# A DLRM tower on one core: five chunks of tile 0 stacked by PE and ACT, and gathers 36 to 95 released by DVE's steps

## The reference

```
e = jnp.stack([tbl_0[ids[:, 0]], ..., tbl_38[ids[:, 38]]], axis=1)   # (2048, 39, 32)
p, q = e[:, ROW, :], e[:, COL, :]                                    # 741 pairs
z = jnp.einsum('bpc,apc,bpa->bp', p, w, q)
h = jnp.concatenate([z, dense_ctx], axis=1)
h = jnp.maximum(h @ W_top1 + b_top1, 0.0)
h = jnp.maximum(h @ W_top2 + b_top2, 0.0)
y = h @ W_top3
```

## Time and profile before

| | |
|---|---|
| time, 3 runs | 738.17, 739.40, 740.45 us; median 739.4 |
| the profiled execution | 739.08 us, its span 737.2 us |
| granted TensorE clock, mean of the span | 0.977 |
| instructions of the span | 10924 |
| DMA traffic | 141.40 MB, mean 192 GB/s |

### The profile page before, as it was taken

The page is one execution under the profiler, slowest core; times in us unless marked ns, Lnnn a source line. Parts: engine busy times, 40 slices in busy tenths (PEclk is TensorE's granted clock), DMA queues, the critical chain, the costliest instruction groups (busy, mean ns, idle before and its releaser), DMA issues.

```text
span 737.2 us, 10924 instructions
## 1 busy us (share of the span) xinstructions
PE 678.2 (92%) x4202; PEld 274.6 (37%) x4202; DVE 608.3 (83%) x773; ACT 104.3 (14%) x186; POOL 415.6 (56%) x424
## 2 busy tenths in 40 slices
PE   0678886898997999999999999999999999999998
PEld 0233332333333444434344444433434444343443
DVE  3776797799996998898889997998889978788740
ACT  3423301111110010101211010110110101011002
POOL 5777465567777766567766665567766666000000
PEclk9888999899998999999999999999999999999999
DMA  7644979779876573547675582728686373553200
GB/s 200 209 119 138 334 272 301 252 231 314 284 227 202 195 257 108 166 140 236 224 225 192 202 281 68 240 85 259 194 270 214 125 254 98 179 174 104 97 0 0
DMA packets 72271, 141.40 MB, mean 192 GB/s; under 512 B 13829, under 2 KB 23704, under 8 KB 72092
## 3 DMA queue, kind: packets, MB, share of 16 engines
q1 hardware_dynamic: 48796, 116.86, 46.2%
q10 hardware_dynamic: 9984, 16.94, 6.4%
q0 software_dynamic: 13440, 6.91, 6.4%
HBM read 109.66 MB, written 31.00 MB: 191 GB/s over the span
## 4 chain that ended last, share of the span: by engine, by line
PE 70%; DVE 14%; issue 7%; DMA 4%; POOL 3%; ACT 1%; SPq 0%; DVEq 0%; ACTq 0%
PE u_ps L593 23%; PE z_ps L617 21%; DVE prod L914 9%; PE m_ps L630 8%; PE t_ps L556 7%; DVE one_hot L902 4%; POOL e_rows L422 3%; PE m_ps L632 3%; PE t_ps L537 2%; DMA e<-scratch 1%; DMA e_rows<-in_tbl_dram,idx 1%; PE u_ps L652 1%; PE u_ps L661 1%; PE m_ps L634 1%; PE t_ps L644 1%
## 5 line engine op out<-in xcount | busy, mean ns | idle before, releaser
L422 POOL DMA_INDIRECT e_rows<-in_tbl_dram,idx x420 | 415.4, 989 | 212.9 <-issue 89.9
L914 DVE TENSOR_TENSOR prod<-u_ps,eT 128x1024 f32<-128x1024 f32 x400 | 469.5, 1216 | 77.6 <-PE u_ps L593 77.1
L593 PE MATMUL u_ps<-e,w 128*128 128x512 f32 x800 | 260.9, 437 | 24.6 <-DVE prod L914 14.6
L617 PE MATMUL z_ps<-prod,sel 128*32 128x512 f32 x1600 | 222.9, 614 | 0.0
L593 PEld LDWEIGHTS u_ps<-e,w 128*128 128x128 f32 x800 | 132.2, 190 | 173.4 <-DVE prod L914 85.9
L902 DVE TENSOR_SCALAR one_hot<-hot_idx,row 125x512 bf16<-125x512 f16 (+2 forms) x296 | 107.6, 420 | 9.6 <-PE t_ps L556 5.8
L556 PE MATMUL t_ps<-one_hot,tb 125*32 125x512 bf16 x1344 | 104.2, 392 | 10.5 <-DVE one_hot L902 9.1
L556 PEld LDWEIGHTS t_ps<-one_hot,tb 125*32 125x32 bf16 x1344 | 43.7, 99 | 89.3 <-issue 57.6
L617 PEld LDWEIGHTS z_ps<-prod,sel 128*32 128x32 f32 x1600 | 33.8, 108 | 111.7 <-issue 87.4
L630 PE MATMUL m_ps<-zT,w1s 128*128 128x512 f32 x144 | 73.5, 592 | 0.0
L720 ACT CAST parts<-t_ps 128x512 fp32r<-128x512 f32 (+1 forms) x40 | 23.4, 586 | 295.4 <-PE t_ps L556 162.4
(11 more groups left out here) (52 smaller groups left out, 122.2 us busy)
## 6 DMA issues: line engine op xcount, KB each, us to landing
w<-w_rows SPq DMA_DIRECT2D x100, 512.0 KB
e<-scratch SPq DMA_DIRECT2D x62, 512.0 KB, 5.7
scratch<-parts SPq DMA_DIRECT2D x62, 256.0 KB
w_rows<-h ACTq DMA_DIRECT2D x48, 256.0 KB
e_rows<-in_tbl_dram,idx POOLq DMA_INDIRECT x420
hot_idx<-hot SPq DMA_DIRECT2D x12, 512.0 KB
h<-in_w_dram ACTq DMA_DIRECT2D x12, 256.0 KB, 4.3
e<-scratch SPq DMA_DIRECT2D x8, 384.0 KB
```

The source lines that it names most:

```text
L422: pool.indirect_dma_start(e_rows[:, r, n, D * q:D * q + D], None, tables[f], bass.IndirectOffsetOnAxis(ap=idx[:, t, f * TPG + n:f * TPG + ...
L593: last = nc.tensor.matmul(u_ps[:, s % 2, place, :], w4[:, p % WR, (u % PW) * P:(u % PW + 1) * P], e4[:, E4_SLOT[g], j - C * g, :], start=T ...
L617: last = nc.tensor.matmul(z_ps[D * quad:D * quad + D, z % 2, :], sel[:, D - 1 - row:2 * D - 1 - row], prod[:, (NS * t + n) % PR, place, :] ...
L914: nc.vector.tensor_tensor(prod[:, s % PR, :, :], u_ps[:, s % 2, :, :], e, ALU.mult).then_inc(s_mul, 1)
```

## The change

Two edits.

1. In tile 0 the stacks of chunks 4, 8, 5, 6 and 9 are no longer stored and read back. PE makes them field by field, one field a batch, from the batches in `FIELD_WISE`, in the bank `m_ps`, and ACT copies each to `e4`. 19 fields: 38 matmuls, 19 copies. Five pairs of stores and five pairs of stack DMAs of SP go. `make_field` stands in PE's order between the batch's `interact` and its `reduce`; it waits for `split_chunk`, and for ACT's copy of the field before it (the bank). `take_field` stands in ACT's order before the batch's `take_z`, `take_chunk` and the weights.
2. Gathers 36 to 95 wait for DVE's steps (36 steps for 60 gathers, from step 1 on) instead of the landing of the gather three before. The rule for the later ones starts from there: gather 96 waits for 37 steps done, 45 before, gather 143 for 80, 88 before, and so on, always 8 fewer.

```diff
@@ -119,8 +119,18 @@
 WR = 4
 ES = 4
 
-PACED_FROM, PACE_LEAD = 96, 52
+PACED_FROM, PACED_FIRST, STEPS_FIRST = 36, 60, 36
 GATHERS_PER_TILE = 108
+
+
+def gather_step(n):
+
+    n -= PACED_FROM
+    if n < PACED_FIRST:
+        return 1 + n * STEPS_FIRST // PACED_FIRST
+    return 1 + STEPS_FIRST + (n - PACED_FIRST) * NS // GATHERS_PER_TILE
+
+
 
 E4_SLOT = {0: 0, 1: 2, 2: 3, 3: 1, 7: 2, 8: 3, 4: 0, 5: 1, 6: 0, 9: 1}
 OS = 3
@@ -151,6 +161,9 @@
 
 MADE = ((0, 1), (0, 0), (0, 2), (0, 3), (0, 7))
 MADE_FIRST = 2
+
+FIELD_WISE = {(0, 4): 9, (0, 8): 15, (0, 5): 21, (0, 6): 30, (0, 9): 35}
+STACKED = MADE + tuple(FIELD_WISE)
 MADE_IN = {1: (((0, 2), 0), ((0, 2), 1)), 4: (((0, 3), 0), ((0, 3), 1)), 5: (((0, 7), 0),), 6: (((0, 7), 1),)}
 MLP_WEIGHTS_BATCH = 7
 LATE = (17, 39)
@@ -189,7 +202,22 @@
 
 def stores_to(n):
 
-    return len([m for m in range(n + 1) if (m - n) % 2 == 0 and ORDER[m] not in MADE])
+    return len([m for m in range(n + 1) if (m - n) % 2 == 0 and ORDER[m] not in STACKED])
+
+
+def stk_at(c, part):
+
+    earlier = STACKED[:STACKED.index(c)]
+    return sum(2 if x in MADE else fields_in(x[1]) for x in earlier) + part + 1
+
+
+def stk_after(c):
+    return stk_at(c, (2 if c in MADE else fields_in(c[1])) - 1)
+
+
+def field_in(b):
+
+    return [(c, b - first) for c, first in FIELD_WISE.items() if first <= b < first + fields_in(c[1])]
 
 
 def halves_before(c, half):
@@ -230,7 +258,7 @@
     INDICES.setdefault(LAST_SLICE.get(LOOKED[LPOS[c] - 2], -1) + 1, []).append(c)
 for b, cs in COMPLETE.items():
     for c in cs:
-        if c in MADE:
+        if c in STACKED:
             continue
         x = e4_before(c)
         free = NBAT * x[0] + J_LAST[x[1]] // UPB + 1 if x else 0
@@ -418,7 +446,7 @@
                             before = issued - WINDOW
                             pool.wait_ge(s_rows[GPOS[GATHERS[before]] % ER][before % WINDOW], landed(before))
                         if issued >= PACED_FROM:
-                            pool.wait_ge(s_mul, PACED_FROM - PACE_LEAD + 1 + (issued - PACED_FROM) * NS // GATHERS_PER_TILE)
+                            pool.wait_ge(s_mul, gather_step(issued))
                         pool.indirect_dma_start(
                             e_rows[:, r, n, D * q:D * q + D], None, tables[f],
                             bass.IndirectOffsetOnAxis(ap=idx[:, t, f * TPG + n:f * TPG + n + 1], axis=0),
@@ -573,6 +601,18 @@
                     for h in range(2):
                         last = nc.tensor.matmul(to, rep[own, 2 - 2 * h:2 - 2 * h + P], parts[own, n % 2, h, :],
                                                 start=h == 0, stop=h == 1)
+                last.then_inc(s_stk, 1)
+
+            def make_field(c, q):
+
+                n = POS[c]
+                pe.wait_ge(s_el, n + 1)
+                d = c if q else STACKED[STACKED.index(c) - 1]
+                pe.wait_ge(s_e4[E4_SLOT[d[1]]], 32 * e4_loads(d) - (32 - 8 * q if q else 0))
+                own = slice(D * q, D * q + D)
+                for h in range(2):
+                    last = nc.tensor.matmul(m_ps[:, :], rep[own, 2 - 2 * h:2 - 2 * h + P], parts[own, n % 2, h, :],
+                                            start=h == 0, stop=h == 1)
                 last.then_inc(s_stk, 1)
 
             def interact(t, n):
@@ -683,6 +723,9 @@
                 for b in range(NBAT):
                     for x in range(SPB):
                         interact(t, SPB * b + x)
+                    if t == 0:
+                        for c, q in field_in(b):
+                            make_field(c, q)
                     if t:
                         for piece in mlp_pieces(b, t == NT - 1):
                             mlp_piece(t - 1, *piece)
@@ -709,8 +752,8 @@
                 n = POS[c]
                 rows = D * fields_in(g)
                 if n >= 2:
-                    if ORDER[n - 2] in MADE:
-                        act.wait_ge(s_stk, 2 * MADE.index(ORDER[n - 2]) + 2)
+                    if ORDER[n - 2] in STACKED:
+                        act.wait_ge(s_stk, stk_after(ORDER[n - 2]))
                     else:
                         act.wait_ge(s_scr[n % 2], 32 * stores_to(n - 2))
                 if hot(c):
@@ -726,7 +769,7 @@
 
             def take_half(c, half):
                 made = MADE.index(c)
-                act.wait_ge(s_stk, 2 * made + half + 1)
+                act.wait_ge(s_stk, stk_at(c, half))
                 x = e4_before(c)
                 if x:
                     act.wait_ge(s_u, step_after(*x))
@@ -736,6 +779,13 @@
                 else:
                     nc.scalar.copy(e4[:, slot, q, :], m_ps[:, :]).then_inc(s_e4[slot], 8)
                     nc.scalar.copy(e4[:, slot, q + 1, :], z_ps[:, 1, :]).then_inc(s_e4[slot], 8)
+
+            def take_field(c, q):
+                act.wait_ge(s_stk, stk_at(c, q))
+                act.wait_ge(s_u, step_after(*e4_before(c)))
+                slot = E4_SLOT[c[1]]
+                rest = 8 if q < fields_in(c[1]) - 1 else 32 - 8 * q
+                nc.scalar.copy(e4[:, slot, q, :], m_ps[:, :]).then_inc(s_e4[slot], rest)
 
             def load_weights(k):
                 a, b = PREP_UNITS[k]
@@ -831,6 +881,9 @@
                         for layer, m, k in mlp_pieces(b, t == NT - 1):
                             if k == LAYER_INPUTS[layer] - 1:
                                 take_mlp(t - 1, layer, m, m_ps[:, :])
+                    if t == 0:
+                        for c, q in field_in(b):
+                            take_field(c, q)
                     for tile in range(NZ):
                         done = ends_tile(tile) // UPB + 1
                         if done == b:
```

## The result

The changed kernel took 734.99 us (median of 20 executions, 730.74 to 740.52); the kernel before, timed beside it, 738.29 (20 executions, 734.78 to 741.08). The ratio is 0.9957, interval 0.9937 to 0.9977: 3.3 us, 0.4% faster. The forecast was 732.3, so less than half of the 7.1 us came. Two executions of the last set of experiments, of 885.82 and 910.98 us, were in a slower state at a lower granted clock, and its medians leave them out. The profiled execution of the changed kernel took 733.83 us (span 732.0), 5.2 us less than the profiled one of before.

A forecast was written before the change was run, and what follows sets the result against it. PE was taken to bound tiles 1 to 3, so only tile 0's idle time could pay. Terms -6.3 - 5.6 + 1.0 + 3.2 + 0.6 = -7.1 us from 739.4 gave 732.3 us, range 727.0 to 737.5.

The forecast's parts named there:

- Rival 1: Tile 0's fields fully exposed, 10.5 instead of 3.2 us: 739.6, half exposed 736; chance 0.12, and 0.03 beyond 739.
- Rival 2: Only one stop goes, another wait replacing it ((1, 0)'s stack or (1, 3)'s gather): price 2.5 to 5.6 us; chance 0.07.
- The two stops: Tile 0, PE's waits at batch 19 (chunk 8's stack) and batch 48 (gather 143) go: -6.3 and -5.6 us.
- The gathers' edit: Gathers 36 to 95 by DVE's steps end POOL's landing waits, so the second stop, batch 48, goes: -5.6 us.
- I count nothing: Some 7 MB of SP's traffic go, spare for the weight loads; counted as 0.
- What is late next: At the second stop, step 100 waits for the stack of (1, 0), still through DRAM: 0 to 4 us, taken as +1.0.
- The fields: 19 fields on PE at 0.55 us, 10.5 us, partly hidden in PE's idle time in batches 9 to 37: +3.2 us exposed.
- ACT's casts: Weight casts stand behind ACT's field copies, so DVE waits, mainly in batches 17 and 37: +0.6 us, bounds 0 and 3.
- The low clock: Low clock after the first stop counted as 0.8 us of its gain; little clock cost expected at the second.
- rival 3: ACT, standing at its weight loads in batches 11, 19, 23, blocks PE's fields: up to +17.2 us, 749.5; chance 0.05.
- Rival 4: More comes than counted, by lighter DMA load and fields at 0.33 us: 728.2, down to 727; chance 0.13.

The follow-up runs named there:

- stacks_only: The changed kernel with only the first edit: five stacks by PE and ACT, gathers as in the kernel before; 734.84 us, ratio 0.9954 to before.
- both_again: The changed kernel, both edits, run once more for a second profile and the granted clock of every timed run; 734.15 us, ratio 0.9956 to before.
- stacks_with_traffic: First edit only, but SP still stores and reads back the five chunks, into memory nobody reads; 737.68 us, ratio 1.0000 to before.
- chunk8_gathers: Changed kernel with both edits, but only chunk 8 made by PE and ACT, chunks 4, 5, 6, 9 through DRAM; 732.25 us, ratio 0.9921 to before.
- chunk8_only: Only chunk 8's stack by PE and ACT, the other four through memory, gathers as in the kernel before; 735.22 us, ratio 0.9968 to before.
- gathers_only: The kernel before with only the second edit: gathers 36 to 95 by DVE's steps, all stacks as before; 734.79 us, ratio 0.9950 to before.

## Why the prediction was right, and where it was wrong

The time lies in the range (727.0 to 737.5) and just inside the forecast's own band, 729.5 to 735. It lies there with some luck: that side of the range was opened for rivals 1 and 2, and neither of them is what took the gain.

**The two stops, right.** -6.3 and -5.6 were forecast, -6.5 and -5.0 measured.

**The gathers' edit, right in effect, wrong in credit.** The step "POOL was late, because of 25 waits for landings" was right; the step that only the second edit ends them was wrong. The same text said that 7 MB of traffic go while the DMA share is 0.87 to 0.98, and "I count nothing". With the stacks alone the waits fell from 33.0 to 19.2 us, and that was enough; put SP's transfers back, and they are back (32.4). For the sum of both edits it made no difference, but the forecast would have been wrong for the first edit alone by the whole second stop, and so were the expectations of stacks_only.

**What is late next: nothing.** +1.0 us for the stack of (1, 0) was forecast; batches 49 and 50 took 8.0 us, as before.

**The fields, right in sum, with their parts off.** +3.2 forecast. At full clock +1.1 in batches 15 to 18 (forecast 1.2), +1.3 with ACT's cast in 35 to 37 (1.1), 0 in 21 to 24 and 30 to 33 (0.9), 0.3 in 9 to 14 (0). Hence 2.7 us with the 0.2 to 0.4 at ACT's casts, for which +0.6 was in the sum. A field held PE for 0.66 us, not 0.55:

```profile
125.23 0.73 PE L614 MATMUL m_ps<-parts,rep 32*128 32x512 f32 x2
125.89 1.07 PE L657 MATMUL z_ps<-prod,sel 128*32 128x512 f32 x8
```

(125.23 to 125.89). Chunks 5's and 6's fields cost nothing because DVE covers them, as the forecast had it for most of their time. The Trainium skill ("TensorE: Matmul & The Clock Gate", Back-to-back issue gap) puts a full-clock matmul of 512 columns at about 216 ns after the one before, by which a field is 0.43 us, an estimate; the trace shows more than either.

**The low clock, missing from the sum.** This is the step that failed. The forecast treated both stops as full gains, put the clock elsewhere at nothing, and took one profile as typical. Without the start and batches 0 to 8 (+2.0) and the low clock in batches 15 and 16 (+1.5) the two profiles differ by -8.7 us; the medians differ by 3.3. Of the 5.4 us between them the runs show this much.

First, low clock in batches 15 to 18 cost 1.5 us beside the fields' 1.1 in the profile of both edits and 4.5 in both_again. Five of the six profiles that have it show the 1.5; before has none there.

Second, part of the low clock of before stood where PE had little to do: 0.66 in the 10 us around the first stop, and at the second

```profile
222.00:230.00 8.00, 3.68 (x18) 2.07 (x18) 2.57 (x3) 0.60 (x2) 6.17 (x7) 0.77 0.74 267
```

The mean clock rose only from 0.977 to 0.979 and 0.980 although both are gone, so more of the low clock stands where PE works.

Third, the profile of before was early: its batch 15 begins at 115.5 us, the mean of the ten profiles in the table is 116.6, and yet its time was 0.8 us above the median.

Some 3 to 4 us stay open. A candidate is that a stop is a buffer: what released the second one came no later when PE was late, so it would give back what was lost ahead of it. For it: in stacks_with_traffic DVE began batch 48 1.7 us earlier than in before, but POOL issued gather 143 at the same time (222.1 and 222.0), and PE's wait grew from 4.1 to 4.6 us. That is 0.4 of the 1.7 us, since the gather landed sooner. And its executions spread by 1.0 us (standard deviation) and by 0.3 us for each 0.001 of their mean granted clock, against 2.1 and 0.7 in stacks_only, which lacks only the transfers. Against it: the other kernels with a stop don't differ from those without. The four with none in the first two sets (both edits, both_again, stacks_only, chunk8_gathers) spread by 2.1 to 2.8 us and by 0.6 to 0.7 us for 0.001, at correlations of -0.96 to -0.98. The kernel before has 2.0 and 2.1 us, 0.7 and 0.6 for 0.001, -0.83 and -0.69 in its two larger sets; chunk8_only 2.3, 0.5 and -0.84; gathers_only 1.5, 0.5 and -0.58. So buffering is argued here and not shown.

**The rivals.** PE waited for no copy of ACT: rival 3 is out, as the forecast had it. Rival 1 is out: the fields cost 2.7 us in all, not 10.5 or half of it. Rival 2 did not come in the changed kernel, where both stops went. Rival 4's lighter DMA load was real (POOL's waits in stacks_only), but brought nothing beside the second edit, and a field took 0.66 us, not 0.33.

## What to carry to other kernels

Here a late gather was cured by taking other transfers out of the stretch, and only by enough of them: chunk 8's alone left the stop. Before adding a second cure, look at what the first one shortens beside its own target. A stop that another chain releases may return what is won or lost ahead of it, so don't count on its idle time in one profile as the gain of removing it. Where executions spread with the granted clock by as much as the gain, one profile on each side is no ledger; compare stretches at equal clock, and medians.

## What the runs showed of the hardware

- In tile 0, with the DMA share at 0.87 to 0.98 in the stretches of the earlier trace rows, some 7 MB less of 141 took 14 us out of POOL's waits for landings of 16 KB gathers (33.0 to 19.2 us in total); chunk 8's transfers alone took 5 us (28.1).
- The time of the changed kernel varied by 10 us over 20 executions (730.74 to 740.52) and followed the mean granted clock (correlation -0.97). Of two profiled executions of it one had a clock of 0.72 in the 6 us around batch 16, the other 0.57 for 12 us.
- One chip took 878 us for the program that took 738 on the others. Chunk 8 on chip with the gathers' edit was worth 3.0% there, 0.8% on another; both edits, with piece 6 moved, 3.0% there, against 0.4% without that move.
